# Moving 64 output columns from plain matmuls into the seven-product block scheme of a tuned LoRA feed-forward kernel

## The chip, the core and the metric

The kernel runs on one core of a Trainium2 chip. The metric is the device time of one execution in microseconds (us). The profile is one further execution, recorded by the hardware profiler. The engines it names: PE is TensorE's matmul stream and PEld its weight loads (the operand that stays in the array), DVE is VectorE, ACT is ScalarE, POOL is GpSimd, SP is SyncE, which here only issues DMAs.

## What is computed

Eight batch elements, each 256 rows of 1024 numbers, all in float32.

```python
w = L0_cond_weight[ids]                       # one of 8 adapters, 1024 x 1024, for each element
y = einsum('bsi,boi->bso', x, w)              # stage 1
base_out = einsum('btd,od->bto', y, base_W) + base_b
logits = einsum('btd,nd->btn', y, router_W) + router_b      # 15 columns
probs = softmax(logits); topk_p, topk_i = top_k(probs, 8)
w = einsum('btk,btke->bte', topk_p, onehot(expert_map[topk_i]))
h = einsum('btd,erd->bter', y, A)             # 8 experts x rank 16 = 128 columns
lora = einsum('bter,eor->bto', h * w[..., None], B) * 2
out = x + base_out + lora                     # stage 2
```

## The kernel before

**Precision.** Every matmul operand is split into a rounded part (`..._hi`, type fp32r, made by ACT) and the remainder (`..._lo`, made by DVE), and three products are summed: hi·hi, hi·lo, lo·hi. Where both parts of the moving operand lie side by side, one matmul covers two of them.

**Stage 1** (`stage1_rows`, `stage1_chunk`) makes y in 8 chunks of 128 output features. A chunk is 8 matmuls of 512 columns with the `w_hi` weights and 8 of 256 with `w_lo`, into one of two banks of `y_ps`. ACT and DVE empty a bank (L389, L541: `y_sum`), and after each odd chunk make `y_hi` (L393) and `y_lo` (L545) of a pair of chunks. So `y_lo` of pair 3, the last, comes after the stage's last matmul. Chunk c may start when DVE has emptied chunk c-2 (`y_sum_done`, L821). The adapter's weights come through a ring of 4 slots (`w_raw`, which lies over `w_lo`, and `w_hi`), 512 KB each.

**Stage 2** has two kinds of work. `plain` (L855) multiplies y by `pl_split`, a matrix of PL columns: 128 of A, 15 of the router, one of padding (AR = 144 together) and NP = 96 columns out of the middle of the base weight. It is 16 matmuls of 2*PL = 480 columns (L863, weights `y_hi`) and 16 of PL = 240 (L866, weights `y_lo`). It runs in two parts: k of 0, 1, 2, 4, 5, 6 for row tile 1, then for tile 0 (24 matmuls), then k of 3 and 7 for tile 1 and for tile 0 (8 matmuls). The second part is the first that needs `y_lo` of pair 3 (L862). The other 928 columns are computed by `product` (L871) from 2 x 2 blocks of NH = 464 columns: elements 1 to 7 use seven block products (a Strassen-like scheme, with sums of blocks in `s_hi`, `s_lo` and in base blocks T1 to T4), 12 matmuls each, 84 in all. Element 0 is computed with eight ordinary block products (96 matmuls), while the sums of base blocks are still being made. `lora_b` adds 12 matmuls of 512 columns, `transposes` 2 of 128. There are 684 product matmuls in the program (96 + 7 x 84).

**Base blocks.** SP loads the four blocks once (L299). In element 0 DVE makes `st_lo` of the first block (L701), then T1 (L710), then `st_lo` of the second block (L701), takes and gating, `st_lo` of T1 (L714), and so on: one instruction per block, 4 x 464 elements per partition. Then POOL makes T2, T3 and T4 by three accumulating DMAs of 928 KB (L994). The first waits for `st_lo` of T1, the third for the first. DVE makes `st_lo` of T2 (L719) when T4 has landed (`t4_in`); in DVE's fixed order that step stands in element 1 between `y_sum` of chunk 0 and the steps for chunk 1. ACT makes `st_hi` of T4 (L455) in element 1 after chunk 6, ahead of its steps for chunks 9 and 7.

**Order.** Each engine runs a list written out by hand, with semaphore waits on exact counts. Nothing is scheduled by a tool. Elements 2 to 6 are a loop.

Of the kernel before, what the change touches and what calls it, by code (L numbers as in the profile page):

```python
# [10 lines left out]
F32R = mybir.dt.float32r  # L11
# [5 lines left out]
P = 128  # L17
W_SLOTS = 4
# [18 lines left out]
def adaln_ffn_kernel(nc, xT, x, ids, wT, a_t, base_t, b_t, router_t, base_b, router_b, expert_map, out):  # L37
    NB, _, KC, T = xT.shape
    OC = wT.shape[1]
    D = KC * P  # L40
    NT = T // P
    ER = b_t.shape[0]
    NR = expert_map.shape[0]
# [2 lines left out]
    AR = ER + NR + 1  # L46
    KH = KC // 2

    NP = 96
    NH = (D - NP) // 2  # L50
    PL = AR + NP
    DH = D // 2
    HALF = NP // 2
    N1, PLAIN, N2 = slice(0, NH), slice(NH, NH + NP), slice(NH + NP, D)
    H1, H2 = slice(0, DH), slice(DH, D)
# [11 lines left out]
    with ExitStack() as ctx:  # L67
# [3 lines left out]
        spot = [SBUF_FROM]  # L71

        def sb(name, shape, dt=F32, over=None):

            size = 4
            for n in shape[1:]:
                size *= n
            offset = spot[0] if over is None else over
            if over is None:
                spot[0] += (size + 31) // 32 * 32  # L80
                assert spot[0] <= SBUF_TO, (name, spot[0])
            return nc.alloc_sbuf_tensor_at(name, shape, dt, offset=offset)
# [8 lines left out]
        at_w = spot[0]  # L91
# [31 lines left out]

        early_raw = [sb(f"early_raw{i}", [P, KC, P], over=at_st + i * 4 * 7 * NH) for i in range(OC - W_SLOTS)]

        at_hwt = spot[0]
        hwt_hi = sb("hwt_hi", [P, NT, P], F32R)
        hwt_lo = sb("hwt_lo", [P, NT, P], F32R)
        hw = sb("hw", [P, NT, ER], over=at_hwt)
        by_expert = sb("by_expert", [P, NT, E, NR], over=at_hwt + 4 * NT * P)  # L130
        router_raw = sb("router_raw", [P, KC, NR], over=at_hwt)
        ident = sb("ident", [P, P])
        ids_sb = sb("ids_sb", [1, NB], I32)
        router_bias = sb("router_bias", [P, NR])
# [13 lines left out]
        marked = sb("marked", [P, NT, NR])  # L148
        gate = sb("gate", [P, NT, E])
        gate_n = sb("gate_n", [P, NT, E])  # L150
        ar_sum = sb("ar_sum", [P, NT, AR])

        def bank(name, shape):
            return ctx.enter_context(nc.psum_tensor(name, shape, F32))
# [894 lines left out]
```

## Time and profile before

| | us |
|---|---|
| median of 3 runs | 401.38 (400.76 to 401.5) |
| the profiled execution | 401.32 |
| its span, first to last instruction | 399.5 |
| DVE busy | 301.2 |
| ACT busy | 159.3 |

The profiled execution lies 1.8 us over its span, and 0.06 us under the median of the runs. A page of the profile gives busy time by engine; the timeline gives single instructions, with start and duration. Matmuls are pipelined, so the recorded duration of one is longer than the time after which the next starts. What a matmul costs is the distance from its start to the next start, here called its spacing.

### The profile page before, as it was taken

Reading aid. Unit: us, or ns where it says so; the run is one execution under the profiler, and the core shown is the slowest. Engines: PE = TensorE matmul, PEld = TensorE weight load, DVE = VectorE, ACT = ScalarE, POOL = GpSimd, SP = SyncE. Lnnn points to the kernel's source line nnn. Section 1 sums busy time; section 2 is a strip of 40 time slices with the busy share of each in tenths; the row PEclk is TensorE's granted clock in tenths of the full one; section 3 lists DMA queues with packets and bytes.
Section 4 is the critical chain, followed back from the end, with each engine's and each line's share of the span. In section 5 each row is a group of like instructions: output and inputs, shape, how many; then the busy total and the mean of one; then the engine's idle time right before and its main releaser. Section 6 shows DMA issues by size and latency. Waiting matters only on the chain.

```text
span 399.5 us, 5965 instructions
## 1 busy us (share of the span) xinstructions
PE 394.5 (99%) x2102; PEld 349.2 (87%) x2102; DVE 301.2 (75%) x553; ACT 159.3 (40%) x226; POOL 11.9 (3%) x22
## 2 busy tenths in 40 slices
PE   8999999999999999999999999999999999999996
PEld 8889888898888988889888888888888898888985
DVE  2877998898968884798657996589846798467763
ACT  3766444672156402554026620355304542144300
POOL 0005210000000000000000000000000000000000
PEclk9999999999999999999999999999999999999999
DMA  7999598830457306653076510775036830464002
GB/s 267 400 393 402 113 199 275 295 111 0 172 197 263 107 0 210 210 216 99 0 263 224 197 51 27 259 275 174 0 91 226 313 105 0 151 219 158 2 0 105
DMA packets 27279, 67.60 MB, mean 169 GB/s; under 512 B 3458, under 2 KB 14338, under 8 KB 27138
## 3 DMA queue, kind: packets, MB, share of 16 engines
q1 hardware_dynamic: 25250, 62.47, 44.0%
q0 software_dynamic: 1872, 3.90, 4.9%
q10 hardware_dynamic: 144, 1.05, 0.7%
q8 instruction: 8, 0.13, 0.1%
q14 instruction: 5, 0.04, 0.0%
HBM read 58.08 MB, written 8.39 MB: 166 GB/s over the span
## 4 chain that ended last, share of the span: by engine, by line
PE 94%; DMA 2%; SPq 1%; DVE 1%; issue 1%; ACT 1%; ACTq 0%
PE y_ps L837 22%; PE y_ps L839 11%; PE pl_ps L863 7%; PE x_ps L877 6%; PE x_ps L878 6%; PE x_ps L876 6%; PE s_ps L877 6%; PE s_ps L878 6%; PE s_ps L876 6%; PE y_ps L825 6%; PE pl_ps L866 4%; PE y_ps L829 3%; DMA early_raw<-in_wT 2%; PE s_ps L891 1%; PE s_ps L893 1%; PE s_ps L892 1%
## 5 line engine op out<-in xcount | busy, mean ns | idle before, releaser
L837 PE MATMUL y_ps<-x_split,w_hi 128*128 128x512 f32 x384 | 133.4, 391 | 0.0
L839 PE MATMUL y_ps<-x_split,w_lo 128*128 128x256 f32 x384 | 107.5, 280 | 0.0
L397 ACT CAST w_hi<-w_raw 128x1024 fp32r<-128x1024 f32 x58 | 60.9, 1051 | 72.2 <-DMA w_raw<-in_wT 72.1
L837 PEld LDWEIGHTS y_ps<-x_split,w_hi 128*128 128x128 f32 x384 | 71.8, 187 | 15.8
L523 DVE TENSOR_TENSOR w_lo<-w_raw,w_hi 128x1024 fp32r<-128x1024 f32 x58 | 70.9, 1224 | 13.8 <-ACT w_hi L397 12.7
L839 PEld LDWEIGHTS y_ps<-x_split,w_lo 128*128 128x128 f32 x384 | 72.6, 189 | 0.3
L389 ACT COPY y_sum<-y_ps 128x256 f32<-128x256 f32 x63 | 23.5, 374 | 61.9 <-PE y_ps L839 50.4
L541 DVE TENSOR_TENSOR y_sum<-y_ps,y_sum 128x256 f32<-128x256 f32 x63 | 26.6, 421 | 18.9 <-ACT y_sum L389 18.6
L863 PE MATMUL pl_ps<-pl_split,y_hi 128*128 128x480 f32 x128 | 32.9, 379 | 0.0
L825 PE MATMUL y_ps<-x_split,w_hi 128*128 128x512 f32 x120 | 30.4, 395 | 0.3 <-DVE y_sum L541 0.2
L876 PE MATMUL s_ps<-st_hi,y_hi 128*128 128x464 f32 x80 | 30.4, 380 | 0.0
L877 PE MATMUL s_ps<-st_lo,y_hi 128*128 128x464 f32 x80 | 29.9, 373 | 0.0
L878 PE MATMUL s_ps<-st_hi,y_lo 128*128 128x464 f32 x80 | 29.7, 372 | 0.0
L635 DVE TENSOR_TENSOR res<-s_ps,res 128x512 f32<-128x512 f32 (+1 forms) x31 | 20.3, 677 | 12.5 <-PE s_ps L893 12.4
L393 ACT CAST y_hi<-y_sum 128x512 fp32r<-128x512 f32 x32 | 20.0, 624 | 21.3 <-DVE y_sum L541 21.3
L545 DVE TENSOR_TENSOR y_lo<-y_sum,y_hi 128x512 fp32r<-128x512 f32 x32 | 22.2, 693 | 6.4 <-ACT y_hi L393 2.7
L825 PEld LDWEIGHTS y_ps<-x_split,w_hi 128*128 128x128 f32 x120 | 21.7, 189 | 4.6 <-issue 0.6
L635 DVE TENSOR_TENSOR res<-x_ps,res 128x512 f32<-128x512 f32 (+1 forms) x15 | 10.0, 668 | 18.8 <-PE x_ps L893 15.4
L877 PE MATMUL x_ps<-st_lo,y_hi 128*128 128x464 f32 x64 | 23.9, 373 | 0.0
L878 PE MATMUL x_ps<-st_hi,y_lo 128*128 128x464 f32 x64 | 23.8, 372 | 0.0
L876 PE MATMUL x_ps<-st_hi,y_hi 128*128 128x464 f32 x64 | 23.8, 372 | 0.0
L863 PEld LDWEIGHTS pl_ps<-pl_split,y_hi 128*128 128x128 f32 x128 | 21.7, 188 | 2.0
(118 smaller groups left out, 618.1 us busy)
## 6 DMA issues: line engine op xcount, KB each, us to landing
w_raw<-in_wT SPq DMA_DIRECT2D x59, 512.0 KB, 3.4
res<-in_x SPq DMA_DIRECT2D x16, 512.0 KB, 4.5
x_raw<-in_xT SPq DMA_DIRECT2D x14, 512.0 KB, 4.8
out<-res SPq DMA_DIRECT2D x13, 512.0 KB, 3.0
early_raw<-in_wT SPq DMA_DIRECT2D x4, 512.0 KB, 8.5
hi_raw<-in_base_t SPq DMA_DIRECT2D x2, 928.0 KB, 10.3
st_raw<-in_base_t SPq DMA_DIRECT2D x2, 928.0 KB, 11.8
st_raw<-in_base_t POOLq DMA_DIRECT2D x2, 928.0 KB, 9.7
```

Source lines behind the costliest of these rows:

```text
L389: nc.scalar.copy(y_sum[:, ORDER[c], :], y_ps[:, c % 2, T:2 * T]).then_inc(y_part_done, 1)
L397: nc.scalar.copy(w_hi[:, c % W_SLOTS, :, :], w_raw[:, c % W_SLOTS, :, :]).then_inc(w_hi_done, 1)
L523: nc.vector.tensor_tensor(w_lo[:, s, :, :], w_raw[:, s, :, :], w_hi[:, s, :, :], ALU.subtract).then_inc(w_lo_done, 1)
L541: nc.vector.tensor_tensor(y_sum[:, o, :], y_ps[:, c % 2, 0:T], y_sum[:, o, :], ALU.add).then_inc(y_sum_done, 1)
L635: return nc.vector.tensor_tensor(res[:, t, cols], ps, res[:, t, cols], ALU.add)
L825: nc.tensor.matmul(y_ps[:, c % 2, :], w_hi[:, s, k, :], x_split[:, k, :, :].rearrange("p s t -> p (s t)"), start=(k == 0), stop=False)
L837: nc.tensor.matmul(y_ps[:, c % 2, :], w_hi[:, s, k, :], x_split[:, k, :, :].rearrange("p s t -> p (s t)"), start=(k == 0), stop=False)
L839: mm = nc.tensor.matmul(y_ps[:, c % 2, 0:T], w_lo[:, s, k, :], x_split[:, k, 0, :], start=False, stop=(k == KC - 1))
L863: nc.tensor.matmul(pl_ps[:, t, 0:2 * PL], y_hi[:, k, t * P:(t + 1) * P], pl_split[:, k, :, :].rearrange("p s n -> p (s n)"), start=(k == 0 ...
L876: nc.tensor.matmul(dst, hi(j), st_hi[:, j, block_of, :], start=begins and j == 0, stop=False, skip_group_check=not begins)
L877: nc.tensor.matmul(dst, hi(j), st_lo[:, j, block_of, :], start=False, stop=False, skip_group_check=not begins)
L878: mm = nc.tensor.matmul(dst, lo(j), st_hi[:, j, block_of, :], start=False, stop=(j == KH - 1), skip_group_check=not begins)
```

## The change

NP goes from 96 to 32, so each of the two base halves has NH = 496 columns in place of 464. Everything whose size derives from them follows: products and their blocks are 496 wide, the plain matmuls are 2*PL = 352 and PL = 176 wide, the block DMAs are 992 KB. The base blocks then take more of the core's memory. So three things move: `hwt_hi`, `hwt_lo` (the transposed gate operand of `lora_b`) and what lies over them (`hw`, `by_expert`) go into the upper half of `w_hi` slot 3, beside `s_hi`, and `router_raw` lies over `ar_sum`. No instruction is added, removed or reordered on any engine, and no wait is added. `w_hi` slot 3 is next written by ACT for chunk 3 of the next element, after `evacuate` of that element's chunk 0.

```diff
-    NP = 96
+    NP = 32
     NH = (D - NP) // 2
     PL = AR + NP
...
-        at_hwt = spot[0]
-        hwt_hi = sb("hwt_hi", [P, NT, P], F32R)
-        hwt_lo = sb("hwt_lo", [P, NT, P], F32R)
+        at_hwt = at_w + (W_SLOTS - 1) * 4 * KC * P + 4 * KH * P
+        hwt_hi = sb("hwt_hi", [P, NT, P], F32R, over=at_hwt)
+        hwt_lo = sb("hwt_lo", [P, NT, P], F32R, over=at_hwt + 4 * NT * P)
         hw = sb("hw", [P, NT, ER], over=at_hwt)
         by_expert = sb("by_expert", [P, NT, E, NR], over=at_hwt + 4 * NT * P)
-        router_raw = sb("router_raw", [P, KC, NR], over=at_hwt)
...
+        at_ar = spot[0]
         ar_sum = sb("ar_sum", [P, NT, AR])
+        router_raw = sb("router_raw", [P, KC, NR], over=at_ar)
```

## Rows read from the trace of the kernel before

**Rows 1.** The page, busy us (share) xinstructions, and the granted clock in tenths.
```profile
PE 394.5 (99%) x2102; PEld 349.2 (87%) x2102; DVE 301.2 (75%) x553; ACT 159.3 (40%) x226; POOL 11.9 (3%) x22
...
PEclk9999999999999999999999999999999999999999
```

**Rows 2.** Waits of PE: who waited for whom, us in total, times, longest.
```profile
PE y_ps L825 <- DVE y_sum L541: 0.2, 1, 0.2
```

**Rows 3.** Timeline of PE, element 1: start us, us, instruction, shapes, xcount.
```profile
81.73 1.47 PE L863 MATMUL pl_ps<-pl_split,y_hi 128*128 128x480 f32 x6
83.03 0.83 PE L866 MATMUL pl_ps<-pl_split,y_lo 128*128 128x240 f32 x6
83.70 1.46 PE L863 MATMUL pl_ps<-pl_split,y_hi 128*128 128x480 f32 x6
...
85.67 0.59 PE L863 MATMUL pl_ps<-pl_split,y_hi 128*128 128x480 f32 x2
...
86.99 0.37 PE L876 MATMUL x_ps<-st_hi,y_hi 128*128 128x464 f32 x1
...
89.52 0.38 PE L876 MATMUL s_ps<-st_hi,s_hi 128*128 128x464 f32 x1
```

**Rows 4.** Timelines of DVE, PEld and PE after an idle moment, then in a full stream.
```profile
19.22 0.42 DVE L541 TENSOR_TENSOR y_sum<-y_ps,y_sum 128x256 f32<-128x256 f32 x1
...
19.75 0.30 PEld L825 LDWEIGHTS y_ps<-x_split,w_hi 128*128 128x128 f32 x2 [0.34 <-issue]
...
19.78 0.47 PE L825 MATMUL y_ps<-x_split,w_hi 128*128 128x512 f32 x1 [0.16 <-DVE y_sum L541]
...
48.06 0.37 PE L878 MATMUL s_ps<-st_hi,y_lo 128*128 128x464 f32 x1
...
48.06 0.19 PEld L876 LDWEIGHTS s_ps<-st_hi,y_hi 128*128 128x128 f32 x1
```

**Rows 5.** Timelines of PE and DVE, element 0, first block product and its operand.
```profile
36.30 0.37 PE L876 MATMUL s_ps<-st_hi,y_hi 128*128 128x464 f32 x1
...
33.36 2.08 DVE L701 TENSOR_TENSOR st_lo<-hi_raw,st_hi 128x1856 fp32r<-128x1856 f32 x1
...
39.37 0.63 DVE L638 TENSOR_TENSOR res<-res,s_ps 128x464 f32<-128x464 f32 x1
```

**Rows 6.** POOL's timeline, DMA landing of L994, then DVE and PE in element 1.
```profile
44.56 1.50 POOL L994 DMA_DIRECT2D st_raw<-in_base_t  x1 [7.01 <-DVE st_lo L714]
48.52 1.30 POOL L994 DMA_DIRECT2D st_raw<-in_base_t  x1 [2.45 <-DVE st_lo L701]
54.11 1.29 POOL L994 DMA_DIRECT2D st_raw<-st_raw  x1 [4.30 <-DMA st_raw<-in_base_t]
...
DMA to landing us min/median/max: 9.1/9.3/10.1
...
63.30 2.09 DVE L719 TENSOR_TENSOR st_lo<-st_raw,st_hi 128x1856 fp32r<-128x1856 f32 x1
...
66.45 0.42 DVE L541 TENSOR_TENSOR y_sum<-y_ps,y_sum 128x256 f32<-128x256 f32 x1
...
67.76 2.00 PE L825 MATMUL y_ps<-x_split,w_hi 128*128 128x512 f32 x8
```

**Rows 7.** Timelines of ACT, DVE and PE at the last pair, elements 1, 2 and 4.
```profile
79.56 1.75 ACT L455 CAST st_hi<-st_raw 128x1856 fp32r<-128x1856 f32 x1
...
84.63 0.69 DVE L545 TENSOR_TENSOR y_lo<-y_sum,y_hi 128x512 fp32r<-128x512 f32 x1
...
131.97 0.69 DVE L545 TENSOR_TENSOR y_lo<-y_sum,y_hi 128x512 fp32r<-128x512 f32 x1
...
133.75 0.59 PE L863 MATMUL pl_ps<-pl_split,y_hi 128*128 128x480 f32 x2
...
228.36 0.69 DVE L545 TENSOR_TENSOR y_lo<-y_sum,y_hi 128x512 fp32r<-128x512 f32 x1
...
229.92 0.60 PE L863 MATMUL pl_ps<-pl_split,y_hi 128*128 128x480 f32 x2
```

## The prediction, made before the changed kernel was run

> **What bounds the kernel now.** I read the page first: PE is busy 99% of the span, the granted clock is full (2.4 GHz) throughout, DVE has 75% and ACT 40% [rows 1]. Then PE's waits: after the first matmul it waits once, 0.2 us [rows 2]. So the time is the sum of matmul spacings plus a little at both ends, and each column removed or added counts. Since PE never waits, every producer is on time, and the second question is by how much: a shorter plain stage brings forward the moments at which its operands are needed. I took the spacings from PE's timeline [rows 3], the time of a weight load from an idle moment [rows 4], and the margins from the timelines of DVE, ACT and POOL [rows 5 to 7].
>
> **Spacings.** 480 columns: (83.03 - 81.73) / 6 = 0.2167 us. 240 columns: (83.70 - 83.03) / 6 = 0.1117. 464 columns: (89.52 - 86.99) / 12 = 0.2108 [rows 3]. Between 240 and 480 that is 0.4375 ns per column, between 464 and 480 0.37. 352 columns lie between measured points: 0.2167 - 128 x 0.4375 ns = 0.1607. 496 lie just outside: 32 columns at 0.37 to 0.4375 ns are 11.8 to 14.0 ns, and I take 13.
>
> 176 columns lie below everything fast in the trace, and here I chose. Carried on, the line gives 0.1117 - 64 x 0.4375 ns = 0.0837. But a matmul needs its weights. In the full stream the load for the next matmul starts with the matmul ahead of it, 48.06 and 48.06. After an idle moment two loads cover 0.30 us and one takes 0.19, so the second starts 0.11 after the first, at 19.86. The second load starts with its preceding matmul, so that matmul really began at 19.86, though its record starts at 19.78 and is 0.47 long: 0.11 after its load, with nothing else on PE [rows 4]. If a load starts only when the matmul ahead starts, and its matmul 0.11 later, no spacing can be under about 0.1095. The 240-column matmuls at 0.1117 would already stand almost on that floor. So for 176 columns: 0.1095 likely, 0.0837 if loads can be closer together than this row shows.
>
> The Trainium skill (TensorE: Matmul & The Clock Gate, "Back-to-back issue gap") gives a gap of N/2.4 + 2.5 ns, 76 ns for 176 columns, which speaks for the lower value; for 240 columns it gives 102.5 ns, and the row has 111.7, so the trace doesn't bear it out. By it the 128 narrow matmuls would save 4.6 us, by the floor 0.3. The same page ("LDWEIGHTS") prices a load at columns / 1.2, 107 ns for 128 columns, near the 0.11 of the row.
>
> **Columns alone, per element.** Plain, wide: 16 x 128 x 0.4375 ns = 0.90 us saved. Plain, narrow: 16 x (0.1117 - 0.1095) = 0.035 saved. Together 0.93, from the 5.26 us between 81.73 and 86.99. Products: 84 x 13 ns = 1.09 us added, in element 0 96 x 13 = 1.25. The columns themselves balance (3072 fewer in plain, 2688 more in products), but the narrow half of plain hardly gives its share back. Elements 1 to 7: +0.16 each. Element 0: +0.32.
>
> **New waits, element 0.** The first product needs `st_lo` of its block. DVE makes it at 33.36, right behind `y_lo` of the last pair, in 2.08 us; 4 x 32 more elements per partition at the rate of this row (2.08 / 1856) are 0.14, taken as 0.13 since a part is fixed. It ends at 35.57. From DVE's end to the load that waits for it is 0.11 (19.64 to 19.75) and to the matmul another 0.11 [rows 4], so the product can begin at 35.79. PE would be there at 36.30 - 0.93 = 35.37 [rows 5]. A wait of 0.42. Later operands of this stage come 0.13 later for each block made, but PE has by then five products of 0.16 more, so I add nothing. Element 0: -0.93 + 0.42 + 1.25 = +0.74.
>
> **Element 1, stage 1.** POOL's three accumulating DMAs run one after the other: issued at 44.56, 48.52 and 54.11, landing 9.3, 10.1 and 9.1 later, at 53.9, 58.6 and 63.2. DVE starts `st_lo` of T2 at 63.30, so it stands at the landing of T4 now, with no margin [rows 6]. The landings are 4.6 to 4.7 us apart, and 992 in place of 928 KB adds 0.32 to each. T1, which releases the first, comes some 0.5 later (three blocks and two narrow takes ahead of it grow; a take is 0.63 for 464 elements [rows 5]), and the first transfer grows by perhaps 0.4. So T4 lands near 64.9 and DVE is free about 1.6 later than before, while PE's stage starts 0.74 later. `y_sum` of chunk 1, at 66.45 for 0.42, stands behind it and gates chunk 3, at 67.76 [rows 6]. It would end near 68.5, the load could go at 68.6, and PE would want it at 67.65 + 0.74 = 68.4. Wait 0.2, and 0.1 at chunk 4: I take 0.3, between 0 (transfers no slower) and 1.2 (DVE's lateness passed on in full).
>
> **Element 1, stage 2.** The second part of plain needs `y_lo` of pair 3. Its load goes at 85.67 - 0.11 = 85.56 now. 12 wide and 12 narrow matmuls ahead of it save 12 x 0.056 + 12 x 0.002 = 0.70, so it would go at 84.86. `y_lo` ends at 84.63 + 0.69 = 85.32, and later by 0.12, since ACT's cast of T4 (79.56, 1.75 us, 7% larger) stands ahead of that chunk's steps [rows 7]; with 0.11 to the load 85.55. Wait 0.69. Element 1: +0.16 + 0.30 + 0.69 = +1.15.
>
> **Elements 2 to 7.** The same step in element 2: load at 133.75 - 0.11 - 0.70 = 132.94, `y_lo` there at 131.97 + 0.69 + 0.11 = 132.77, no wait. Element 4, the tightest: 229.92 - 0.81 = 229.11 against 228.36 + 0.80 = 229.16, wait 0.05 [rows 7]. The others lie like element 2 or better. Together 6 x 0.16 + 0.05 = +1.01.
>
> **Free edits.** The gate operand in slot 3 adds no semaphore, and ACT's next write there stands behind a step that waits for PE's next element, so it costs nothing. `router_raw` is read before `ar_sum` is first written. The last adds and the last store keep their shapes. DVE's takes grow by 0.03 each, its plain adds shrink.
>
> **Sum.** 0.74 + 1.15 + 1.01 = +2.9 us. Against the profiled execution, 401.32 (span 399.5), that is 404.2. The median of the runs, 401.38, is 0.06 away, which I leave aside.
>
> **Rivals.** (a) **No floor under the spacing.** A 176-column matmul takes 0.084. Plain is then 1.34 shorter, and elements 2 to 7 gain 0.25 each, 1.5. But the waits grow: element 0 is still held to 35.79 (+0.74), element 1's stage 2 waits 1.0, elements 2, 3, 5 wait 0.14 each, element 6 0.2, element 4 0.36. Sum 0.74 + 0.30 + (-0.25 + 1.0) - 1.5 + 1.0 = +1.3: 402.6. For it: nothing shorter was tried in a stream. Against: the idle moment in [rows 4]. (b) **Faster: columns alone decide.** As (a), but DVE's last pair and the first block are ready in time, because those chains were only as fast as PE let them be. Element 0 changes by -0.09, seven elements by -0.25: -1.8, 399.5. It needs a narrow spacing under 0.0995, where 0.90 + 16 x (0.1117 - s) equals 1.09, and no new wait at all; [rows 5] and [rows 7] show DVE running back to back into both points, so it needs two readings to be wrong. (c) **Floor, but no waits.** 0.32 + 7 x 0.16 = +1.4: 402.8. (d) **The T4 chain costs its upper end**, or a further operand is late in the first two elements: 1 us more and beyond, 405.2 and up. (e) **The change doesn't do what it says**: a reused place could make a hidden wait; nothing in the semaphores shows one.
>
> **How the numbers follow.** Forecast 0.58, (a) 0.12, (b) 0.05, (c) 0.08, (d) 0.15, (e) 0.02. This measurement can tell about 0.2%, 0.8 us, from no change. Faster by more than that is (b): 0.05. Within it lie the low edge of (a) and parts of (b) and (c): 0.08. Slower: 0.87. The forecast's own range comes from the 496-column price (684 x 1.1 ns = 0.75 either way) and from 0 to 1.2 for T4: 403.1 to 405.6. To hold the time 8 times in 10 it reaches down over (a) and (c): 402.4 to 405.8.
>
> **What would show it.** In the timeline of the changed kernel: six narrow matmuls of plain in 0.66 (floor) or 0.50; six wide in 0.96; twelve product matmuls in 2.69. PE's waits, nearly empty now, should list one on DVE's `st_lo` in element 0 (0.4) and one on `y_lo` in element 1 (0.7), and one on `y_sum` in element 1's stage 1. The six long elements should each be about 0.16 longer from start to start. If narrow matmuls run at 0.084, or if PE's waits stay empty, the forecast is wrong.

## The result, and the profile after

The changed kernel takes 406.56 us (406.48 to 406.94, 4 runs). The kernel before, beside it on the same chip, takes 401.07 (400.26 to 401.5). The ratio is 1.0139, with a 95% interval of 1.0126 to 1.0153: slower by 5.5 us, where the prediction had +2.9 and at most 405.8, which is +4.4. The profiled execution of the changed kernel is 406.51 with a span of 404.7; that of before has 401.32 and 399.5. So the spans differ by 5.2 us.

The lines of the changed file lie one lower: L838 and L840 are the wide and the narrow matmul of stage 1, L864 and L867 those of plain, L877 to L879 the products. First the page of the changed kernel, busy times, then two groups of PE (busy, mean ns | idle before):

```profile
PE 399.4 (99%) x2102; PEld 345.3 (85%) x2102; DVE 300.8 (74%) x553; ACT 159.2 (39%) x226; POOL 12.0 (3%) x22
...
L838 PE MATMUL y_ps<-x_split,w_hi 128*128 128x512 f32 x384 | 135.9, 399 | 0.0
...
L864 PE MATMUL pl_ps<-pl_split,y_hi 128*128 128x352 f32 x128 | 26.6, 329 | 0.2 <-DVE y_lo L546 0.2
```

And the wide matmuls of stage 1 in the kernel before:

```profile
L837 PE MATMUL y_ps<-x_split,w_hi 128*128 128x512 f32 x384 | 133.4, 391 | 0.0
```

PE is 4.9 us busier than in [rows 1], with the same 2102 matmuls. Plain got cheaper, as meant. But the wide matmuls of stage 1 show 2.5 us more, and **the change doesn't touch their shape, count or order**. The waits of PE and its weight loads in the changed kernel (us in total, times, longest), where [rows 2] had one:

```profile
PEld pl_ps L864 <- DVE y_lo L546: 0.4, 1, 0.4
...
PEld s_ps L877 <- DVE st_lo L702: 0.3, 1, 0.3
...
PE pl_ps L864 <- DVE y_lo L546: 0.2, 1, 0.2
...
PE y_ps L826 <- DVE y_sum L542: 0.2, 1, 0.2
...
PEld y_ps L826 <- ACT w_hi L398: 0.2, 1, 0.2
```

The waits on `y_lo` and on `st_lo` are two that the prediction named. The one of PE on `y_sum` is not: it lies at 18.94 us, in element 0, where [rows 2] has it too. The third named wait is the last line, at 70.59 us in element 1 (more on it below). All are single events under half a microsecond and can't hold 5.2 us. So I laid the timelines of PE side by side, from the start of one stage to the start of the next. Element 3 before (start of stage 1, plain, products, next element):

```profile
155.72 0.39 PE L837 MATMUL y_ps<-x_split,w_hi 128*128 128x512 f32 x1
...
177.91 0.59 PE L863 MATMUL pl_ps<-pl_split,y_hi 128*128 128x480 f32 x2
...
183.15 0.37 PE L876 MATMUL x_ps<-st_hi,y_hi 128*128 128x464 f32 x1
...
203.79 0.39 PE L837 MATMUL y_ps<-x_split,w_hi 128*128 128x512 f32 x1
```

and after, with the rows of plain:

```profile
157.25 0.39 PE L838 MATMUL y_ps<-x_split,w_hi 128*128 128x512 f32 x1
...
179.86 1.14 PE L864 MATMUL pl_ps<-pl_split,y_hi 128*128 128x352 f32 x6
180.83 0.81 PE L867 MATMUL pl_ps<-pl_split,y_lo 128*128 128x176 f32 x6
181.48 1.15 PE L864 MATMUL pl_ps<-pl_split,y_hi 128*128 128x352 f32 x6
...
184.20 0.41 PE L877 MATMUL x_ps<-st_hi,y_hi 128*128 128x496 f32 x1
...
206.06 0.39 PE L838 MATMUL y_ps<-x_split,w_hi 128*128 128x512 f32 x1
```

Stage 1 went from 22.19 to 22.61 us, plain from 5.24 to 4.34, the rest from 20.64 to 21.86. It is the same in elements 2 to 7, to about 0.01 us. Worked out from such rows for the whole program, in us:

| stretch of PE | before | after | change | predicted |
|---|---|---|---|---|
| up to plain of element 0 | 31.03 | 30.20 | -0.83 | 0 |
| rest of element 0 | 28.37 | 29.12 | +0.75 | +0.74 |
| element 1, stage 1 | 22.32 | 22.56 | +0.24 | +0.30 |
| element 1, rest | 25.90 | 26.57 | +0.67 | +0.85 |
| elements 2 to 7, stage 1, each | 22.190 | 22.608 | +0.42 | 0 |
| plain, each | 5.249 | 4.341 | -0.91 | -0.93 |
| products and low rank, each | 20.64 | 21.86 | +1.22 | +1.09 |

The six stage 1 stretches alone make +2.5. The question for the experiments is why unchanged matmuls take longer. Their single spacings show how. Before, from one wide matmul of stage 1 to the third after it:

```profile
155.94 0.28 PE L839 MATMUL y_ps<-x_split,w_lo 128*128 128x256 f32 x1
156.06 0.40 PE L837 MATMUL y_ps<-x_split,w_hi 128*128 128x512 f32 x1
...
157.10 0.39 PE L837 MATMUL y_ps<-x_split,w_hi 128*128 128x512 f32 x1
```

After:

```profile
157.48 0.28 PE L840 MATMUL y_ps<-x_split,w_lo 128*128 128x256 f32 x1
157.60 0.40 PE L838 MATMUL y_ps<-x_split,w_hi 128*128 128x512 f32 x1
...
158.66 0.40 PE L838 MATMUL y_ps<-x_split,w_hi 128*128 128x512 f32 x1
```

Three pairs (512 columns with `w_hi`, 256 with `w_lo`) take 1.04 us before and 1.06 after: 346.7 ns a pair against 353.3. Before, each pair is 230 + 117 ns. After, three kinds of pair alternate: 233 + 117, 241 + 120, 236 + 113. Elements 2 to 7 have 384 such pairs, and 384 x 6.6 ns are the 2.5 us. Nobody waits there, and the granted clock is full. I call these the two rhythms, of 346.7 and of 353.3; the expectations below call them the fast and the slow one.

### The profile page after: what moved, and what is told of

The parts are those of the page before. It is cut to its first block, busy times and chain, and to the rows that moved or that the text cites. A ratio compares the mean times of both kernels' runs of the same rounds, so it can differ in the third digit from the quotient of the medians.

```text
span 404.7 us, 5965 instructions
## 1 busy us (share of the span) xinstructions
PE 399.4 (99%) x2102; PEld 345.3 (85%) x2102; DVE 300.8 (74%) x553; ACT 159.2 (39%) x226; POOL 12.0 (3%) x22
## 4 chain that ended last, share of the span: by engine, by line
PE 94%; DVE 2%; ACT 1%; DMA 1%; issue 1%; SPq 0%; ACTq 0%
PE y_ps L838 22%; PE y_ps L840 11%; PE x_ps L877 7%; PE x_ps L878 7%; PE x_ps L879 7%; PE s_ps L877 6%; PE y_ps L826 6%; PE s_ps L878 6%; PE s_ps L879 6%; PE pl_ps L864 4%; PE y_ps L830 3%; PE pl_ps L867 3%; PE s_ps L892 1%; PE s_ps L894 1%; PE s_ps L893 1%; PE y_ps L853 1%
## 5 line engine op out<-in xcount | busy, mean ns | idle before, releaser
L838 PE MATMUL y_ps<-x_split,w_hi 128*128 128x512 f32 x384 | 135.9, 399 | 0.0
L840 PE MATMUL y_ps<-x_split,w_lo 128*128 128x256 f32 x384 | 107.8, 281 | 0.0
L838 PEld LDWEIGHTS y_ps<-x_split,w_hi 128*128 128x128 f32 x384 | 72.2, 188 | 18.0
L840 PEld LDWEIGHTS y_ps<-x_split,w_lo 128*128 128x128 f32 x384 | 72.5, 189 | 0.2
L877 PE MATMUL s_ps<-st_hi,y_hi 128*128 128x496 f32 x80 | 31.7, 396 | 0.1
L878 PE MATMUL s_ps<-st_lo,y_hi 128*128 128x496 f32 x80 | 31.0, 387 | 0.0
L879 PE MATMUL s_ps<-st_hi,y_lo 128*128 128x496 f32 x80 | 30.9, 386 | 0.0
L826 PE MATMUL y_ps<-x_split,w_hi 128*128 128x512 f32 x120 | 30.5, 396 | 0.2 <-DVE y_sum L542 0.2
L864 PE MATMUL pl_ps<-pl_split,y_hi 128*128 128x352 f32 x128 | 26.6, 329 | 0.2 <-DVE y_lo L546 0.2
L877 PE MATMUL x_ps<-st_hi,y_hi 128*128 128x496 f32 x64 | 24.9, 390 | 0.0
L878 PE MATMUL x_ps<-st_lo,y_hi 128*128 128x496 f32 x64 | 24.8, 387 | 0.0
L879 PE MATMUL x_ps<-st_hi,y_lo 128*128 128x496 f32 x64 | 24.8, 387 | 0.0
L879 PE MATMUL x_ps<-st_hi,s_lo 128*128 128x496 f32 x56 | 21.6, 386 | 0.0
```

Source lines behind the costliest of these rows:

```text
L826: nc.tensor.matmul(y_ps[:, c % 2, :], w_hi[:, s, k, :], x_split[:, k, :, :].rearrange("p s t -> p (s t)"), start=(k == 0), stop=False)
L838: nc.tensor.matmul(y_ps[:, c % 2, :], w_hi[:, s, k, :], x_split[:, k, :, :].rearrange("p s t -> p (s t)"), start=(k == 0), stop=False)
L840: mm = nc.tensor.matmul(y_ps[:, c % 2, 0:T], w_lo[:, s, k, :], x_split[:, k, 0, :], start=False, stop=(k == KC - 1))
L864: nc.tensor.matmul(pl_ps[:, t, 0:2 * PL], y_hi[:, k, t * P:(t + 1) * P], pl_split[:, k, :, :].rearrange("p s n -> p (s n)"), start=(k == 0 ...
L877: nc.tensor.matmul(dst, hi(j), st_hi[:, j, block_of, :], start=begins and j == 0, stop=False, skip_group_check=not begins)
L878: nc.tensor.matmul(dst, hi(j), st_lo[:, j, block_of, :], start=False, stop=False, skip_group_check=not begins)
```

## The experiments

Times of a single run are given without an interval; each stands beside the kernel before, measured with it. "Stage 1" is the mean of elements 2 to 7 and tells the rhythm: 22.19 us is 346.7, 22.60 is 353.3.

**e1_place: the new places, the old widths.** The gate operand and the router weights stay where the change put them; products and plain get their old shapes. Against the changed kernel:

```diff
-    NP = 32
+    NP = 96
```

> The changed kernel with NP back at 96, so all shapes are those of the kernel before, but the gate operand stays in weight slot 3 and the router weights over ar_sum. Two theories on why the 512- and 256-column matmuls of stage 1, whose shapes and addresses didn't change, take 353.3 ns a pair in elements 2 to 7 after the change and 346.7 before. Placement theory (where the later buffers lie in SBUF decides): 353.3 a pair here too, about 2.5 us over the kernel before. Phase theory (the rhythm in which the preceding matmuls hand over to stage 1 decides): 346.7 a pair, and the time of the kernel before within 0.2%.

400.75 us against 400.74, ratio 0.9999 (0.9987 to 1.0011). From the start of stage 1 of element 3 to plain:

```profile
156.43 0.39 PE L838 MATMUL y_ps<-x_split,w_hi 128*128 128x512 f32 x1
...
178.62 0.38 PE L864 MATMUL pl_ps<-pl_split,y_hi 128*128 128x480 f32 x1
```

22.19: the rhythm of before. The places cost nothing and don't touch stage 1. **The widths do.** (This execution had a wait of 1.0 us on `y_lo` in element 1, so a profiled execution of these shapes isn't always as free of waits as the one in [rows 2].)

**e2_np64: half the change.** `NP = 64`: products 480, plain 416 and 208.

> The changed kernel with NP = 64: products of 480 columns, plain matmuls of 416 and 208. By columns, against the kernel before: wide plain 16 x 64 x 0.4375 ns = 0.45 us less an element, narrow plain 16 x 2 ns = 0.03 less (weight-load floor of 0.1095), products 84 x 16 x 0.434 = 0.58 more, so +0.10 an element, in all +0.9, plus at most 0.5 of waits in elements 0 and 1. The phase theory says nothing sure of stage 1: 346.7 or 353.3 a pair, or a third value. If a third value, then it isn't a choice between two states. So 402.0 to 402.5 with the fast rhythm, 404.5 to 405 with the slow one. Without a floor under the narrow matmuls it would be 0.4 less an element.

405.3 us against 400.74, ratio 1.0116 (1.0082 to 1.0149).

```profile
156.62 0.39 PE L838 MATMUL y_ps<-x_split,w_hi 128*128 128x512 f32 x1
...
179.22 0.35 PE L864 MATMUL pl_ps<-pl_split,y_hi 128*128 128x416 f32 x1
```

22.60. Half the change has the whole loss in stage 1. Its plain is 4.80 and its rest 21.29, both about halfway. So it is a switch, not a cost per column.

**e3_lo144: is there a floor?** The narrow matmuls of plain lose their 32 base columns, 176 to 144 (this part of the product with `y_lo` is left out).

```diff
-  mm = nc.tensor.matmul(pl_ps[:, t, 0:PL], ..., pl_split[:, k, 0, :],
+  mm = nc.tensor.matmul(pl_ps[:, t, 0:AR], ..., pl_split[:, k, 0, 0:AR],
```

> The changed kernel with the 128 narrow plain matmuls cut from 176 to 144 columns (the y_lo part of the 32 plain base columns is left out). Floor theory: spacing stays near 0.110, the time stays within 0.3 us of the changed kernel. Without a floor 128 x 32 x 0.4375 ns = 1.8 us less. A side effect: if the rhythm of stage 1 hangs on what runs ahead of it, it may change here as well, which would be seen in the 353.3 a pair.

407.94 us against 400.74. Six narrow matmuls:

```profile
182.30 0.79 PE L867 MATMUL pl_ps<-pl_split,y_lo 128*128 128x144 f32 x6
182.93 1.17 PE L864 MATMUL pl_ps<-pl_split,y_hi 128*128 128x352 f32 x6
```

0.63 us, against 0.65 (180.83 to 181.48) for six of 176. That looks like 3 ns less each, but it all lies in the first of the six: from the second on, five take (182.93 - 182.37) / 5 = 0.112, as with 176 columns.

```profile
182.37 0.72 PE L867 MATMUL pl_ps<-pl_split,y_lo 128*128 128x144 f32 x5
```

And what the first is ahead, the wide matmul behind the six gives back: its spacing is 0.205, where it is 0.19 in the changed kernel and 0.16 in a run of wide ones. From one stage 1 to the next, elements 3 to 6 of both kernels take the same 48.81 us. **The floor is there: 32 columns fewer give nothing.** The total is 1.4 above that of the changed kernel because `y_lo` was waited for in two elements (plain 5.155 and 5.492). Stage 1 stayed at 22.608.

**e4_rows: the same matmuls of stage 1 in rows.** Element 1 already runs each chunk as eight wide, then eight narrow. Here all elements do.

```diff
-            def element(b, rows=False):
+            def element(b, rows=True):
```

(One more line changes, so that a special case of element 0 stays with element 0.)

> The changed kernel with stage 1 of elements 2 to 7 issued as eight wide matmuls, then eight narrow, as elements 0 and 1 are, instead of wide and narrow in turn. If the slow rhythm belongs to the alternation, a chunk takes 2.79 us as in element 1 (2.793 there), not 2.826, so 8 x 0.033 x 6 = 1.6 us less than the changed kernel, 404.9. If something slows stage 1 from outside (other engines' traffic, placement), chunks stay at 2.82 or above and the time at 406.5 or more.

404.81 us against 400.74. Element 3:

```profile
156.98 0.39 PE L826 MATMUL y_ps<-x_split,w_hi 128*128 128x512 f32 x1
...
179.33 0.33 PE L864 MATMUL pl_ps<-pl_split,y_hi 128*128 128x352 f32 x1
```

22.34, where the interleaved order has 22.19 or 22.60. A chunk in rows takes 2.793 us in every kernel here, the changed one and that of before. Only the interleaved order has two rhythms, 2.774 or 2.826 a chunk. The whole is 1.75 below the changed kernel, where 6 x 0.26 = 1.6 come from stage 1.

**f1_p464: the old width of the products.** Plain stays at 352 and 176; the product matmuls and DVE's adds run over 464 columns (32 columns of every block are left out of the output).

```diff
-    nc.tensor.matmul(dst, hi(j), st_hi[:, j, block_of, :], ...)
+    nc.tensor.matmul(dst, hi(j), st_hi[:, j, block_of, 0:464], ...)
```

> The changed kernel (all its buffers, loads and splits 496 wide, plain 352 and 176) with the product matmuls and DVE's adds of their results cut to 464 columns, so 32 columns of each block are left out of the output. Products should return to 0.2103 a matmul: 684 x 13.9 ns = 9.5 us less. For stage 1: if the spacing follows from the widths that run ahead of it, a pair may return to 346.7 ns (then another 2.5 us less, 394.5); if it follows from where the buffers lie, it stays at 353.3 (397).

396.91 us against 400.88. Starts of stage 1, plain, products and the next element:

```profile
155.68 0.39 PE L839 MATMUL y_ps<-x_split,w_hi 128*128 128x512 f32 x1
...
177.87 0.32 PE L865 MATMUL pl_ps<-pl_split,y_hi 128*128 128x352 f32 x1
...
182.19 0.40 PE L878 MATMUL x_ps<-st_hi,y_hi 128*128 128x464 f32 x1
...
202.88 0.39 PE L839 MATMUL y_ps<-x_split,w_hi 128*128 128x512 f32 x1
```

22.19 again. So it is the width of the products, ahead of stage 1, that switches the rhythm, and not plain or the transfers of stage 1. It also gives the price of 32 product columns: (21.86 - 20.70) / 84 = 13.8 ns. The time is 2.4 above the 394.5 that was expected with this rhythm. The trace has it all in the first two elements: against the changed kernel 0.4 more ahead of plain, the rest of element 0 only 0.16 shorter in place of 1.3 (PE waited for `st_lo`), and stage 1 of element 1 0.85 longer (PE waited for `y_sum`).

**f2_after_extra, f3_before_extra: one small matmul at the entry.** A matmul of 32 columns, overwritten at once by the first of chunk 0, ahead of stage 1 of elements 2 to 7; in f2 in the changed kernel, in f3 in the kernel before.

```diff
                 pe.wait_ge(y_sum_done, OC * b + c - 1)
+                if c == 0:
+                    nc.tensor.matmul(y_ps[:, 0, 0:32], w_hi[:, s, 0, :], x_split[:, 0, 0, 0:32], start=True, stop=True)
```

> The changed kernel with one extra matmul of 32 columns, overwritten at once, ahead of chunk 0 of stage 1 in elements 2 to 7. Its own cost is one weight load, 6 x 0.11 = 0.7 us. Phase theory (the rhythm of the pairs depends on the moment at which the stream enters it): the pairs may change over to 346.7 ns, then 0.7 - 2.5 = 1.8 us less than the changed kernel. If the rhythm is fixed by something that lasts (placement, program), 353.3 a pair stays and the time is 0.7 more.

> The kernel before with the same extra matmul. Phase theory: the pairs may change over to 353.3 ns or keep 346.7; with 353.3 the time is 0.7 + 2.5 = 3.2 us over the kernel before. Lasting cause: 346.7 stays, 0.7 us over the kernel before.

f2: 408.35 us, stage 1 22.69, still the rhythm of 353.3. f3: 404.78 against 400.88 of before without it. Its element 3:

```profile
156.48 0.18 PE L837 MATMUL y_ps<-x_split,w_hi 128*128 128x32 f32 x1
156.50 0.48 PE L839 MATMUL y_ps<-x_split,w_hi 128*128 128x512 f32 x1
...
179.20 0.38 PE L865 MATMUL pl_ps<-pl_split,y_hi 128*128 128x480 f32 x1
```

22.69, the pairs at 353.3: 0.50 more in each of six elements, of which the extra matmul itself can hold only some 0.09. **The kernel before, with its own widths, falls into the rhythm of 353.3** through one matmul at the entry. (The other 0.9 of its 3.9 us goes with a wait on `y_lo` in element 1, where plain took 6.34 and not 5.26.)

**g1_after_extra256, g2_after_extra416: other widths at the entry.** As f2, with 256 and 416 columns.

> The changed kernel with the extra matmul ahead of chunk 0 widened from 32 to 256 columns (elements 2 to 7), which shifts the stream's entry into the pairs by another amount, near 0.12 us. Phase theory: among three entry shifts (none, 32 and 256 columns) some should give 346.7 ns a pair; if this one does, 6 x (0.12 - 0.42) = 1.8 us less than the changed kernel, about 404.7. If it stays at 353.3 it is 0.7 more.

> The same with 416 columns, near 0.19 us. Phase theory: another draw; with 346.7 ns a pair 6 x (0.19 - 0.42) = 1.4 us less, about 405.1; with 353.3, 1.1 more. If neither this nor the 256-column one changes the rhythm, the entry alone doesn't explain it in the changed kernel, and the slow rhythm is simply the common one.

408.53 and 408.21 us against 401.15, stage 1 22.61 in both, the rhythm of 353.3. None of the three widths brought the changed kernel back.

**g3_last464: only the last product.** The last of the seven products ahead of stage 1 is cut to 464 columns in elements 1 to 7 (32 columns of it are left out); the six others stay at 496.

```diff
-                product(x_ps, y_block(1, 1), T4, begins=False)
+                product(x_ps, y_block(1, 1), T4, begins=False, n=464)
```

> The changed kernel with only the last product of each of elements 1 to 7 (the T4 product, 12 matmuls) cut to 464 columns, so 32 columns of it are left out of the output. Columns: 7 x 12 x 13.9 ns = 1.2 us less. Phase theory: only the last matmuls ahead of stage 1 differ, so the rhythm may change to 346.7 (then 2.5 more off, 402.8); with 353.3 it is 405.3.

403.52 us against 401.15.

```profile
157.43 0.39 PE L838 MATMUL y_ps<-x_split,w_hi 128*128 128x512 f32 x1
...
179.62 0.32 PE L864 MATMUL pl_ps<-pl_split,y_hi 128*128 128x352 f32 x1
```

22.19. Twelve matmuls, followed by three of 512, decide the rhythm of the next 128. The rest is 0.19 shorter (21.67 against 21.86) and stage 1 0.42, together 3.7 over six elements; g3 is 3.0 below the changed kernel, and the stage 1 of its element 1 was 0.5 longer.

**h2_after_vlate, h3_before_vlate: the same work in another order.** In g3 work is left out. Here nothing is: the three matmuls of the low-rank part into `v_ps` go behind the T4 product instead of ahead of it. h2 does it in the changed kernel, h3 in the kernel before.

```diff
-                lora_b(1, v_ps, H2, begins=True).then_inc(v_ps_done, 1)
                 pe.wait_ge(t_lo_done, 4)
                 pe.wait_ge(x_added, x_adds(b, 3))
                 product(x_ps, y_block(1, 1), T4, begins=False)
+                lora_b(1, v_ps, H2, begins=True).then_inc(v_ps_done, 1)
```

> The changed kernel with the three lora_b matmuls into v_ps moved behind the T4 product, so that six of 512 columns precede stage 1, not three. All work is kept. Phase theory: the entry shifts, so the rhythm may be 346.7 ns a pair, 2.5 us less than the changed kernel (404.0); or stay at 353.3 with the same time. Fast rhythm here would show that order alone can pay back the stage 1 part of the loss.

> The kernel before with the same three matmuls moved. The same instructions in another order. Phase theory: the rhythm may fall to 353.3 ns a pair, 2.5 us slower than the kernel before, with nothing added; or stay.

Both went over to the other rhythm, in opposite directions. h2, stage 1 of element 3 to plain:

```profile
158.50 0.40 PE L838 MATMUL y_ps<-x_split,w_hi 128*128 128x512 f32 x1
...
180.68 0.32 PE L864 MATMUL pl_ps<-pl_split,y_hi 128*128 128x352 f32 x1
```

h3:

```profile
155.91 0.39 PE L837 MATMUL y_ps<-x_split,w_hi 128*128 128x512 f32 x1
...
178.51 0.38 PE L863 MATMUL pl_ps<-pl_split,y_hi 128*128 128x480 f32 x1
```

22.18 and 22.60. In h2 the mean of a pair is 346.7 ns as in the kernel before, but the pattern is a third one: 233 + 117 and 231 + 113 in turn. h3 takes 403.71 us against 400.9: **2.8 us for three matmuls in another place.** Stage 1 holds 6 x 0.41 = 2.5 of it, and one wait on `y_lo` in element 2 another 0.19. h2 takes 405.6 and so gains only 1.0 us on the changed kernel, not 2.5. Its stage 1 of element 1 took 23.42, 0.87 more, with this wait of DVE behind the T4 landing, and this one of PE behind DVE; another 0.8 lie in element 0, 0.3 of it ahead of plain and 0.5 behind:

```profile
DVE st_lo L720 <- DMA st_raw<-st_raw: 1.4, 1, 1.4
```

and

```profile
69.10 2.09 PE L826 MATMUL y_ps<-x_split,w_hi 128*128 128x512 f32 x8 [0.48 <-DVE y_sum L542]
```

**f4_t4_late, g4_rows_t4late, h1_before_t4late: the wait on `y_lo`.** ACT casts T4 ahead of the last chunks of element 1 [rows 7]. Here the cast goes to the end of ACT's list of that element: in the changed kernel (f4), together with rows (g4), and in the kernel before (h1).

```diff
-                    if isinstance(b, int) and b == 1 and c == 6:
-                        act.wait_ge(t4_in, 16)
-                        nc.scalar.copy(st_hi[:, :, T4, :], st_raw[:, :, T4, :]).then_inc(t4_hi_done, 1)
...
                 fourth_hi(b)
+                if isinstance(b, int) and b == 1:
+                    act.wait_ge(t4_in, 16)
+                    nc.scalar.copy(st_hi[:, :, T4, :], st_raw[:, :, T4, :]).then_inc(t4_hi_done, 1)
```

> The changed kernel with ACT's cast of T4 in element 1 moved from after chunk 6 to the end of ACT's list for that element. If that cast is what makes y_lo of pair 3 late in element 1, y_lo comes 1.7 us earlier, PE's wait on it (0.4 us) goes, and the plain stage of element 1 takes 4.34 us as in the others, not 4.76. Nothing else moves: 0.4 us less than the changed kernel. If the wait has another cause, the plain stage stays at 4.76.

> The changed kernel with stage 1 in eight wide, then eight narrow matmuls in every element (chunk 2.793 us instead of 2.826) and with ACT's cast of T4 at the end of element 1's list. Against the kernel before, by the traces: elements 2 to 7 plain -0.92, products +1.20, stage 1 +0.155 each, so +2.6, element 0 +0.75, element 1 +0.7 to 1.0: ratio about 1.010 (404.9), below the changed kernel's 1.0139 and above the kernel before. If the slow stage 1 were the whole of the loss, the ratio would be within 0.2% of 1.

> The kernel before with only ACT's cast of T4 moved to the end of its list for element 1. In traces of kernels with the old widths PE sometimes waits 1 us for y_lo of pair 3 in element 1 (two of three traces), where the margin is 0.25 us. If that cast feeds the wait, the wait goes and the kernel is up to 0.5 us faster on average (0.1%); if weight loads alone make it, no difference. Rhythm of stage 1: 346.7 ns a pair, since nothing that PE issues is changed.

f4: 407.65 us against 400.88, the wait on `y_lo` larger (0.78 us in element 1, 0.42 in the changed kernel), not gone. Its chain began elsewhere, with a transfer of weights that landed late; the row of ACT behind it:

```profile
76.65 1.05 ACT L398 CAST w_hi<-w_raw 128x1024 fp32r<-128x1024 f32 x1 [1.16 <-DMA w_raw<-in_wT]
```

So f4 says nothing for or against the cast: what moved `y_lo` there was a landing. g4: 405.22 against 401.15, ratio 1.0100 (1.0062 to 1.0138). Element 1 had no wait, but element 2 had one, and its plain took 5.21 in place of 4.33.

h1: 400.75 us (12 runs) against 400.9 (17 runs), ratio 0.9991 (0.9978 to 1.0005). In its trace `y_lo` of element 1 is 0.68 us ahead of its load where it was 0.25 ahead, but since that margin was positive already, nothing that can be told from zero came of it.

**Does the rhythm belong to the kernel or to the execution?** f1, f3, g3, h2 and h3 have one execution each. Within each, all six elements agree. And the kernel before, run 42 times in all beside these kernels, never took more than 402.6 us; the rhythm of 353.3 would add 2.5 to its median of 400.7 to 401.2. The traces with the old widths and nothing moved on PE (before, e1, h1) all have 346.7, those with the new ones (after, e3, f4) all 353.3. So chance between executions is unlikely as the cause, but for the five kernels it isn't excluded.

All runs together, us; stage 1, plain and rest are means over elements 2 to 7, and plain is given without the elements that waited:

| kernel | products / plain | stage 1 | plain | rest | time | before beside it |
|---|---|---|---|---|---|---|
| before | 464 / 480, 240 | 22.190 | 5.249 | 20.64 | 401.07 | |
| changed | 496 / 352, 176 | 22.608 | 4.341 | 21.86 | 406.56 | 401.07 |
| e1_place | 464 / 480, 240 | 22.190 | | | 400.75 | 400.74 |
| e2_np64 | 480 / 416, 208 | 22.600 | 4.800 | 21.29 | 405.3 | 400.74 |
| e3_lo144 | 496 / 352, 144 | 22.608 | 4.319 | 21.88 | 407.94 | 400.74 |
| f1_p464 | 464 / 352, 176 | 22.190 | 4.319 | 20.70 | 396.91 | 400.88 |
| g3_last464 | 496, last 464 / 352, 176 | 22.190 | | 21.67 | 403.52 | 401.15 |
| h2_after_vlate | as changed, reordered | 22.187 | 4.328 | 21.87 | 405.6 | 400.9 |
| h3_before_vlate | as before, reordered | 22.600 | | | 403.71 | 400.9 |
| f3_before_extra | as before, entry matmul | 22.691 | | | 404.78 | 400.88 |
| f2_after_extra | as changed, entry matmul | 22.691 | | | 408.35 | 400.88 |
| g1_after_extra256 | as changed, entry matmul | 22.61 | 4.341 | 21.86 | 408.53 | 401.15 |
| g2_after_extra416 | as changed, entry matmul | 22.61 | 4.327 | 21.86 | 408.21 | 401.15 |
| e4_rows | as changed, rows | 22.344 | 4.325 | 21.86 | 404.81 | 400.74 |
| g4_rows_t4late | as e4, cast of T4 late | 22.344 | 4.325 | 21.86 | 405.22 | 401.15 |
| f4_t4_late | as changed, cast of T4 late | 22.608 | 4.341 | 21.86 | 407.65 | 400.88 |
| h1_before_t4late | as before, cast of T4 late | 22.190 | 5.249 | 20.64 | 400.75 | 400.9 |

No kernel of this study that does the whole work beats the kernel before. The best that the runs suggest for these widths is the changed kernel in the rhythm of 346.7: an estimate of 404 from 406.56 - 2.5, which no run reached. The kernel before remains ahead, since 0.91 us of plain doesn't pay for 1.22 us of products.

## Why the prediction was wrong, point by point

**The direction was right**, two of the three named waits stood where they were placed, and most terms were near:

- *The spacings.* Wide: predicted 0.1607, measured (180.83 - 179.86) / 6 = 0.162. Narrow: predicted 0.1095 by the floor. Six together give (181.48 - 180.83) / 6 = 0.108, but that mixes two things. The first goes at the pace of its columns, 180.83 to 180.92; the other five take (181.48 - 180.92) / 5 = 0.112. Their weight loads are as far apart, (181.39 - 180.83) / 5 = 0.112:

```profile
180.92 0.72 PE L867 MATMUL pl_ps<-pl_split,y_lo 128*128 128x176 f32 x5
...
180.83 0.64 PEld L867 LDWEIGHTS pl_ps<-pl_split,y_lo 128*128 128x128 f32 x5
181.39 0.78 PEld L864 LDWEIGHTS pl_ps<-pl_split,y_hi 128*128 128x128 f32 x5
```

  The wide matmul behind the six has a spacing of 0.19 in place of 0.16, and so gives back what the first was ahead. (The last narrow run does the same to the first product, 0.253 in place of 0.225.) In sum a narrow matmul costs 0.112, as much as one of 240 columns: the 0.035 that the prediction gave it is nothing. The way to the floor holds: in no trace does a load start before the matmul ahead of it, nor less than 0.107 after the load ahead of it. Plain, by its own stretch, gave 0.91 an element where 0.93 was predicted; 0.03 of that comes back at the first product. Rival (a), no floor, falls with this and with e3. The value that I worked out by the Trainium skill (TensorE: Matmul & The Clock Gate, "Back-to-back issue gap"), 76 ns for 176 columns, isn't borne out as a cost: 144 columns, for which the formula gives 62.5, stand at 112 as well. The page calls this formula the gap of a single matmul, which leaves the weight load out. Its 107 ns for a weight load ("LDWEIGHTS") fits the least distance of two loads, 0.107.
- *Element 0, rest.* +0.74 predicted, +0.75 measured. The match is partly luck: 96 product matmuls cost 96 x 13.9 ns = 1.33 more and not 1.25, and PE began sooner behind DVE than expected. DVE's block is 0.14 longer, as said. It ends at 34.74; the load of the product starts at 34.79 and the next load, which marks the real start of the product's matmul, at 34.90: 0.16 behind DVE and not 0.22.

```profile
32.52 2.22 DVE L702 TENSOR_TENSOR st_lo<-hi_raw,st_hi 128x1984 fp32r<-128x1984 f32 x1
...
34.79 0.49 PE L877 MATMUL s_ps<-st_hi,y_hi 128*128 128x496 f32 x1
```

- *Element 1, stage 1.* +0.30 predicted (0.2 at chunk 3, 0.1 at chunk 4), +0.24 measured, all at chunk 4. The T4 chain is behind it, by another link. DVE waits 0.46 for the landing, but T4 came at 63.58, not near 64.9 (0.83 of the difference is the early start, 0.5 a chain of transfers that was taken too slow). So `y_sum` of chunk 1 ends at 67.28, in time for chunk 3. But ACT's `y_hi` and then its `w_hi` for chunk 4 wait for it, DVE's `w_lo` for that `w_hi`, and behind `w_lo` DVE makes `y_sum` of chunk 2, 70.06 to 70.48, for which chunk 4 waits. (The list names ACT's `w_hi` instead: that is a cast for chunk 5, which happened to end at 70.53.) The other runs had between 0 and 1.1 us here over the kernel before (1.10 in h2), so the bounds of 0 and 1.2 were about right and the single value is one draw from them.

```profile
63.58 2.22 DVE L720 TENSOR_TENSOR st_lo<-st_raw,st_hi 128x1984 fp32r<-128x1984 f32 x1 [0.46 <-DMA st_raw<-st_raw]
```

- *Element 1, stage 2.* The wait is where it was placed, 0.42 in size and not 0.69. Two steps of it were too dear: from the end of a DVE instruction to the load that it releases are 0.05 us here, and not the 0.11 that I took from one row of [rows 4]; and the 0.12 of delay by ACT's cast didn't come: `y_lo` ended 3.54 us behind the start of plain, where it had been 3.59.

```profile
84.73 0.69 DVE L546 TENSOR_TENSOR y_lo<-y_sum,y_hi 128x512 fp32r<-128x512 f32 x1
...
85.47 0.43 PE L864 MATMUL pl_ps<-pl_split,y_hi 128*128 128x352 f32 x1 [0.20 <-DVE y_lo L546]
```

**What failed** is the step "The columns themselves balance ... Elements 1 to 7: +0.16 each". Behind it stood the assumption that a matmul's spacing depends on its own columns alone, so that the stages whose shapes don't change keep their time. The plain and product terms held, but stage 1 took 0.42 us more in each of elements 2 to 7: +2.5 us, by itself more than the whole miss of 2.3 in the span. From start to start such an element grew by 0.73 us, where 0.16 was predicted. e1 excluded the new places, f1 put it on the width of the products, g3 showed that the last twelve of them are enough, and h2 and h3 showed that order alone, with nothing else changed, switches the rhythm both ways. Why the stream takes one or the other stays open. No rival of the prediction had this mechanism.

**What was mis-sized** is the price of 496 columns: 13.9 ns over 464 (13.8 by f1), not 13. Over 684 matmuls that is +0.6 us, inside the range that I had given it (11.8 to 14). The bounds of 0.75 for this price and 0 to 1.2 for T4 add up to 403.1 and 405.8, not 405.6; the measured time lies above either.

**What I didn't foresee and got as a present** is 0.83 us at the start. The 26 warm-up matmuls, before (first row) and after (second), take:

```profile
1.49 5.92 PE L970 MATMUL s_ps<-ident 128*128 128x128 f32 x26 [1.49 <-POOL ident L987]
```

```profile
1.49 4.84 PE L971 MATMUL s_ps<-ident 128*128 128x128 f32 x26 [1.49 <-POOL ident L988]
```

The spacing is 0.213 us at first and falls to 0.111 after the 17th in the changed kernel; in the one before all 26 stand at 0.213. The halving would fit 1.2 and 2.4 GHz, but the trace's granted clock is full in that stretch too, so no run shows the cause. The same row takes 5.02 us in e1_place, 5.30 in h1_before_t4late and 5.89 in h2_after_vlate, so it belongs to the execution and not to the change. In the comparison of profiles it hid 0.8 us of the loss.

In sum, from the table: +2.90 predicted, +2.51 for the rhythm, +0.75 for the products and low rank and +0.08 for plain in elements 2 to 7, -0.23 for elements 0 and 1, -0.83 for the start make +5.18 of the span; measured were 5.2. Without the early start, which is luck, the miss would be larger by 0.8.

## What to carry to other kernels

In a kernel where PE never waits, don't assume that an untouched stream keeps its spacing. Compare the spacing of unchanged matmuls ahead of anything else when a change's time doesn't add up: 6.6 ns a pair is invisible in any wait and made half the loss here. A stream that alternates wide and narrow matmuls had two rhythms in this kernel, chosen at its entry, while the same matmuls grouped by width had one (22.34 against 22.19 or 22.60); the grouped order is the one whose time can be forecast. And narrowing a matmul below 240 columns gave nothing here, where each has its own weights: 144, 176, 208 and 240 columns all cost 0.112 us. To see it, don't divide a short run's length by its count; look at the single spacings, and at the first matmul behind the run.

## What the runs showed of the hardware that I hadn't expected

- **Two rhythms of one stream.** Pairs of 512 and 256 columns, each with new weights, in fp32r, at the full granted clock: 346.7 ns (230 + 117 constantly, or in h2 two pairs in turn) or 353.3 ns (a pattern of three pairs). The rhythm holds for all 64 pairs of a stage and in all six elements. The last 12 product matmuls ahead of it (496 or 464 columns), three low-rank matmuls before or behind them, or, in the kernel before, one matmul of 32 columns at the entry, decide which. Extra matmuls of 32, 256 and 416 columns did not bring the changed kernel back.
- **What sets it stays open.** It looks like a phase that the stream keeps once it has it, but I could not say beforehand which entry leads where. The weight loads don't tell the rhythms apart: each starts 2 to 3 ns behind the matmul ahead of it in the kernel before and 2 to 5 ns in the changed one. "Phase" describes the rows and is not a shown cause.
- **The floor.** Matmuls that each load new weights stand at 0.112 us for 144, 176, 208 and 240 columns, the warm-up's of 128 at 0.111 to 0.112 once they are fast. A recorded start can be too early: behind a short matmul the record of the next begins 0.08 after its load (176 columns) or 0.065 (144), and is as much longer.
- **Margins move between executions.** The landings of T4 and of the weights gave waits of 0 to 1.15 us in elements 1 and 2, also between kernels with the same shapes and order there (before and e1: none and 1.0 us on `y_lo`). A single execution's margin of 0.25 us in [rows 7] is not a margin to count on.
